# Eight of sixteen 64x64 products moved to the crosswise corners of the array, and the order of three VectorE pieces changed

## The reference

```python
qkvz = x @ W_qkvz                      # 16 key heads, each with q, k and 2 value heads, z
q, k, v = silu(causal_conv1d(...))     # 4 taps
g = cumsum(-exp(A_log) * softplus(a + dt_bias))      # within a chunk of 64 tokens
attn = -(k_beta @ k.T * decay_mask)    # strictly lower, 64x64, for each chunk and value head
for i in 1..63: attn[i] += attn[i] @ attn            # forward substitution
attn = attn + I                        # the inverse of (I - the strict lower part)
for each chunk c:                      # a recurrence over 8 chunks
    v_new = attn_c @ (v_beta - (k_beta * exp(g)) @ state)
    out_c = (q @ state) * exp(g) + tril(q @ k.T * decay) @ v_new
    state = state * exp(g_last) + (k * decay).T @ v_new
out = rmsnorm(out * silu(z)) @ W_out
```

## Time and profile before

| | |
|---|---|
| median of 3 runs | 5113.57 us (5109.58 to 5119.2) |
| the profiled execution | 5113.86 us |
| its span | 5112.0 us |
| PE busy | 4816.1 us, 94% |
| DVE busy | 3623.3 us, 71% |
| ACT busy | 3030.3 us, 59% |
| POOL busy | 1086.1 us, 21% |
| granted TensorE clock, whole span | 0.99 of full speed |

### The profile page before, as it was taken

How to read it: one execution, slowest core, us unless ns; L and a number is a source line. 1 busy time by engine, 2 the same in 40 slices (tenths; PEclk the granted TensorE clock), 3 DMA queues, 4 the chain that set the end, 5 groups by cost and what they waited for, 6 DMA issues and landing times.

```text
span 5112.0 us, 140221 instructions
## 1 busy us (share of the span) xinstructions
PE 4816.1 (94%) x52272; PEld 3343.4 (65%) x52272; DVE 3623.3 (71%) x6423; ACT 3030.3 (59%) x7915; POOL 1086.1 (21%) x1064
## 2 busy tenths in 40 slices
PE   4998999999999999999999999999999999999998
PEld 2555666666666666666666666666666666666666
DVE  7554777777777677777777777777776777777775
ACT  2333665666666566666666566666666666666665
POOL 0000222222222222222222222222222222222222
PEclk9998999999999999999999999999999999999999
DMA  2111222222222222222222222222222222222221
GB/s 59 40 43 55 65 59 55 57 61 63 59 53 74 69 59 56 56 61 63 60 53 73 70 59 54 58 61 63 59 53 71 68 62 53 58 63 57 65 52 35
DMA packets 686356, 300.71 MB, mean 59 GB/s; under 512 B 599152, under 2 KB 642288, under 8 KB 675440
## 3 DMA queue, kind: packets, MB, share of 16 engines
q1 hardware_dynamic: 546416, 283.18, 21.7%
q10 hardware_dynamic: 139264, 8.42, 1.8%
HBM read 212.76 MB, written 66.07 MB: 55 GB/s over the span
## 4 chain that ended last, share of the span: by engine, by line
issue 50%; PE 25%; POOL 12%; DVE 6%; DMA 3%; ACT 2%; ACTq 1%; SPq 1%; POOLq 0%; DVEq 0%
POOL sdec L1514 5%; PE pj L653 4%; POOL rout L1520 4%; PE dsb L790 2%; PE pot L598 2%; POOL kn L1507 2%; PE pj L648 2%; PE ms L711 2%; PE pot L748 2%; PE ms L582 1%; PE dsb L762 1%; PE pj L582 1%; PE pot L719 1%; POOL gb L1502 1%; ACTq L332 1%
## 5 line engine op out<-in xcount | busy, mean ns | idle before, releaser
L1261 DVE SCALAR_TENSOR_TENSOR cy<-xpad,cw,cy 128x1024 f32<-128x1024 f32 x768 | 1105.1, 1446 | 8.6 <-ACT cy L974 1.6
L653 PE MATMUL pj<-xnT,wt 128*128 128x512 f32 x2048 | 1021.2, 622 | 25.9 <-DMA xnT<-xnT_d 14.3
L1520 POOL TENSOR_TENSOR rout<-rin,expo 128x2 f32<-128x2 f32 x512 | 359.0, 701 | 2336.9 <-DVE rin L1402 2336.9
L1514 POOL TENSOR_TENSOR sdec<-st,gel 128x512 f32<-128x512 f32 x384 | 402.9, 1049 | 1149.5 <-DVE st L1391 970.2
L653 PEld LDWEIGHTS pj<-xnT,wt 128*128 128x128 f32 x2048 | 351.4, 191 | 355.5 <-issue 340.8
L790 PE MATMUL dsb<-wo,yT 128*128 128x256 f32 x2048 | 573.5, 402 | 8.0 <-issue 7.0
L973 ACT ACTIVATE xpad<-pj 128x512 f32<-128x512 f32 x512 | 304.1, 594 | 376.0 <-PE pj L653 376.0
L648 PE MATMUL pj<-wt,xnT 128*128 128x256 f32 x2048 | 510.2, 392 | 0.0
L1032 ACT ACTIVATE yT<-dsb 128x256 f32<-128x256 f32 x512 | 196.6, 384 | 522.3 <-PE dsb L781 522.1
L1391 DVE TENSOR_TENSOR st<-dsb,sdec 128x512 f32<-128x512 f32 x384 | 265.3, 691 | 312.9 <-PE dsb L762 312.7
L965 ACT ACTIVATE arena<-pj 128x512 f32<-128x512 f32 x256 | 152.9, 597 | 468.4 <-issue 320.3
(11 more groups left out here) (166 smaller groups left out, 8453.7 us busy)
## 6 DMA issues: line engine op xcount, KB each, us to landing
qge<-ge_rows SPq DMA_DIRECT2D x64, 1024.0 KB, 7.0
wt<-in_L_attn_W_qkvz SPq DMA_DIRECT2D x64, 768.0 KB, 4.6
gb<-g_rows SPq DMA_DIRECT2D x128, 256.0 KB, 4.1
a_d<-at SPq DMA_DIRECT2D x64, 512.0 KB, 2.6
wo<-in_L_attn_W_out SPq DMA_DIRECT2D x64, 256.0 KB, 2.7
x_d<-xpair SPq DMA_DIRECT2D x128, 128.0 KB, 1.8
ap_<-a_d SPq DMA_DIRECT2D x512, 16.0 KB, 1.8
dd<-x_d SPq DMA_DIRECT2D x512, 16.0 KB, 2.0
```

The source lines that it names most:

```text
L653: last = mm(pj[n % 2][:, :], wt[:, k, col:col + DH], batch(xnT, k, i), start=(k == 0), stop=(k == KD - 1))
L1261: stt(y, x[:, :, tap:tap + SEQ], cw[:, kind, tap:tap + 1], y, ALU.mult, ALU.add).then_inc(S["conv"], 1)
L1514: tt(sdec[:, :, :, :], st[:, c % 2, :, :, :], bc(gel[:, p, :, :].rearrange("p h (b c) -> p b h c", b=NB)[:, :, :, c], 3, DH), ALU.mult).th ...
L1520: tt(rout[:, :], rin[:, :], expo[:, 0, 0:GRP], ALU.pow).then_inc(S["routs"], 1)
```

## The change

1. Of the 16 units, the last eight go crosswise: unit 8 + v of sequence b enters the array from its own rows (b) but leaves by the columns of the other half (1 - b). So one loop step uses all four 64x64 corners: the straight product of unit v writes bank ms0, the turned product of unit 8 + v writes ms1. A turned operand lies in the other half of the partitions in the next round: odd steps turn it, even ones turn it back. That wants two more tiles: `pback`, the off x dd products of units 8 to 15 unturned, and `eturn`, their ee in the other half.
2. For `pback`, 16 more products stand in slot 19, in the two straight corners, into bank pj1 (`off_products_back`), and a third `negated` copy of 512 columns on ACT. For `eturn`, SP issues eight more DMAs of 8 KB after those of `dd`.
3. The two halves of a step are one loop now: PE waits for both additions of a round before it, and both `yp` signals come at its end.
4. On DVE the first product of the join moves from slot 14 to slot 12 (`join_first`); `join_right` and `turn_inverse` stay in slot 15 but stand right behind `residual` (`front_urgent`); `decayed_squares` of q moves from slot 15 to slot 18, also right behind `residual`; the taps of the value heads move from slots 17, 17, 18, 18, 20, 21 to 15, 15, 17, 17, 18, 20.
5. On ACT `squares` of q moves behind the ring's copies of slot 10, and `silu` of the second value head from slot 22 to 21.

```diff
-                        ("kk", 2), ("pp", 2), ("yp", 6),
+                        ("kk", 2), ("pp", 3), ("yp", 6),
...
+                loaded(sp, d_x1, g, 1)
+                apart(sp)
+                for r in range(GRP * NBLK):
+                    turned = (r + NBLK) % (GRP * NBLK)
+                    sp.dma_start(eturn[turned * BLK:(turned + 1) * BLK, :, (r % NBLK) * BLK:(r % NBLK + 1) * BLK],
+                                 x_d[r * U + U // 2:(r + 1) * U, 1].rearrange("u j i -> j u i")).then_inc(d_et, 16)
...
+            def tile_product(out, b, lhsT, rhs, a):
+                return mm(out, lhsT, rhs, start=True, stop=True, tile_position=(a * CH, b * CH))
+
-            def off_products(g, p, n):
-                if n == 0:
-                    loaded(pe, d_dd, g, GRP * NBLK)
-                    loaded(pe, d_off, g, NB * (NBLK - 1))
-                    after(pe, "atit", g, 2)
-                else:
-                    after(pe, "coef", g, 5)
+            def off_products(g, p):
+                loaded(pe, d_dd, g, GRP * NBLK)
+                loaded(pe, d_off, g, NB * (NBLK - 1))
+                after(pe, "atit", g, 2)
+                after(pe, "coef", g, 5)
                 apart(pe)
                 for v in range(8):
-                    u = 8 * n + v
+                    cut = slice(v * CH, (v + 1) * CH)
                     for b in range(NB):
-                        last = mm(ms[n][half(b), v * CH:(v + 1) * CH], off[half(b), u, :], dd[half(b), u, :],
-                                  start=True, stop=True, tile_position=(b * CH, b * CH))
-                last.then_inc(S["pp"], 1)
+                        straight = tile_product(ms[0][half(b), cut], b, off[half(b), v, :], dd[half(b), v, :], b)
+                        turned = tile_product(ms[1][half(1 - b), cut], 1 - b, off[half(b), 8 + v, :],
+                                              dd[half(b), 8 + v, :], b)
+                straight.then_inc(S["pp"], 1)
+                turned.then_inc(S["pp"], 1)
+
+            def off_products_back(g, p):
+                after(pe, "pcopy", g, RING - 4)
+                apart(pe)
+                for v in range(8):
+                    for b in range(NB):
+                        last = tile_product(pj[1][half(b), v * CH:(v + 1) * CH], b, off[half(b), 8 + v, :],
+                                            dd[half(b), 8 + v, :], b)
+                last.then_inc(S["pp"], 1)
...
+            def fixpoint(g, p, r):
                 if r == 0:
                     loaded(pe, d_ee, g, GRP * NBLK)
-                    after(pe, "pneg", g, n + 1)
+                    loaded(pe, d_et, g, GRP * NBLK)
+                    after(pe, "pneg", g, 2)
                 else:
-                    after(pe, "yadd", g, 2 * (r - 1) + n + 1)
+                    after(pe, "yadd", g, 2 * r)
+                    if r == 1:
+                        after(pe, "pneg", g, 3)
...
+                        straight = tile_product(ms[0][half(b), cut], b, pbd[half(b), v, :], src[half(b), v, :], b)
+                        if r == 1:
+                            turned = tile_product(ms[1][half(1 - b), cut], 1 - b, pback[half(b), v, :],
+                                                  yy[half(b), 8 + v, :], b)
+                        else:
+                            rhs = yy[half(1 - b), 8 + v, :] if r else eturn[half(1 - b), v, :]
+                            turned = tile_product(ms[1][half(b), cut], b, pbd[half(1 - b), 8 + v, :], rhs, 1 - b)
+                straight.then_inc(S["yp"], 1)
+                turned.then_inc(S["yp"], 1)
...
                 if s == 10:
                     silu(g, p, 1)
-                    squares(g, p, 1)
...
+                if s == 10:
+                    squares(g, p, 1)
...
-                for n, at_s in enumerate((2, 3, 3, 8, 8, 9, 17, 17, 18, 18, 20, 21)):
+                for n, at_s in enumerate((2, 3, 3, 8, 8, 9, 15, 15, 17, 17, 18, 20)):
...
+            def front_urgent(g, hk, s):
+                if s == 15:
+                    join_right(g)
+                    turn_inverse(g)
+                if s == 18:
+                    decayed_squares(g, hk % 2, 1)
...
                     if c:
                         residual(g, p, c)
+                    urgent(3 * c)
```

More of the change, by code:

```diff
@@ L108, in build @@
         pbd = sb("pbd", [P, U, CH])
+        pback = sb("pback", [P, U // 2, CH])
+        eturn = sb("eturn", [P, U // 2, CH])
         st = sb("st", [P, 2, NB, GRP, DH])
@@ L204, in build @@
         d_w, d_g, d_ge, d_wo, d_q = sem("d_w"), sem("d_g"), sem("d_ge"), sem("d_wo"), sem("d_q")
[L205 removed]
+        d_a0, d_a, d_off, d_x0, d_x1, d_dd, d_ee, d_et = (sem(n) for n in ("d_a0", "d_a", "d_off", "d_x0", "d_x1", "d_dd", "d_ee", "d_et"))
         phase = sem("phase")
@@ L708, in fixpoint @@
                 for v in range(8):
-                    u = 8 * n + v
+                    cut = slice(v * CH, (v + 1) * CH)
                     for b in range(NB):
-                        last = mm(ms[n][half(b), v * CH:(v + 1) * CH], pbd[half(b), u, :], src[half(b), u, :],
-                                  start=True, stop=True, tile_position=(b * CH, b * CH))
-                last.then_inc(S["yp"], 1)
+                        straight = tile_product(ms[0][half(b), cut], b, pbd[half(b), v, :], src[half(b), v, :], b)
[5 more added lines that the diff above has]
+                            turned = tile_product(ms[1][half(b), cut], b, pbd[half(1 - b), 8 + v, :], rhs, 1 - b)
@@ L806, in front_piece @@
                     chunk_squares(g, p, 1)
-                for n in range(2):
-                    if s == 19:
-                        off_products(g, p, n)
-                for n, at_s in enumerate((20, 20, 22, 22, 23, 23)):
+                if s == 19:
+                    off_products(g, p)
+                    off_products_back(g, p)
+                for r, at_s in enumerate((20, 22, 23)):
                     if s == at_s:
-                        fixpoint(g, p, n // 2, n % 2)
+                        fixpoint(g, p, r)
                 for n in range(RING - 2, RING):
@@ L1008, in negated @@
                     before(act, "yp", g)
-                fn(pbd[:, 8 * n:8 * n + 8, :], ms[n][:, :].rearrange("p (u c) -> p u c", u=8), ACT.Copy, scale=-1.0
+                fn(pbd[:, 8 * n:8 * n + 8, :] if n < 2 else pback[:, :, :],
+                   (ms[0], ms[1], pj[1])[n][:, :].rearrange("p (u c) -> p u c", u=8), ACT.Copy, scale=-1.0
                    ).then_inc(S["pneg"], 1)
@@ L1041, in front_piece @@
                     silu(g, p, 1)
-                    squares(g, p, 1)
                 if s == 16:
                     output_weights(g, p)
-                for n in range(2):
+                for n in range(3):
                     if s == 19:
@@ L1106, in done_then @@
                 dve.wait_ge(s, n)
-            for t in (xpad, dd, ee, off, xpair):
+            for t in (xpad, dd, ee, eturn, off, xpair):
                 dve.memset(t[:], 0.0)
@@ L1369, in add_round @@
                 src = ms[n][:, :].rearrange("p (u c) -> p u c", u=8)
+                add = eturn[:, :, :] if (r, n) == (1, 1) else ee[:, us, :]
                 if r < 2:
-                    tt(yy[:, us, :], src, ee[:, us, :], ALU.add).then_inc(S["yadd"], 1)
+                    tt(yy[:, us, :], src, add, ALU.add).then_inc(S["yadd"], 1)
                 else:
@@ L1427, in front_piece @@
                     invert_rows(g, 5, 8)
+                    join_first(g)
                 if s == 14:
                     join_left(g)
-                if s == 15:
-                    join_right(g)
-                    turn_inverse(g)
-                    decayed_squares(g, p, 1)
-                for n, at_s in enumerate((2, 3, 3, 8, 8, 9, 17, 17, 18, 18, 20, 21)):
+                for n, at_s in enumerate((2, 3, 3, 8, 8, 9, 15, 15, 17, 17, 18, 20)):
                     if s == at_s:
@@ L1439, in front_piece, with core @@
                         add_round(g, p, n // 2, n % 2)
-            def core(g, hk, fill=lambda s: None, first=False):
+            def front_urgent(g, hk, s):
[4 more added lines that the diff above has]
+                    decayed_squares(g, hk % 2, 1)
+            def core(g, hk, urgent=lambda s: None, fill=lambda s: None, first=False):
                 p = hk % 2
@@ L1468, in front @@
                 for s in range(3 * NC):
+                    front_urgent(g, hk, s)
                     front_piece(g, hk, s)
             def weave(g, hk, first=False):
-                core(g, hk, lambda s: front_piece(g + 1, (hk + 1) % HK, s), first)
+                core(g, hk, lambda s: front_urgent(g + 1, (hk + 1) % HK, s),
+                     lambda s: front_piece(g + 1, (hk + 1) % HK, s), first)
             meet(dve, 1)
```

16 lines of the change are left out of this document (8 added, 8 removed).

## The result

The changed kernel took 4975.6 us (median, 4973.1 to 4981.6); the kernel before, run beside it, 5111.6. The ratio is 0.9735, with a 95% interval of 0.9718 to 0.9752: 136 us faster, where I had forecast 170. The profiled execution took 4975.1, its span 4973.3.

A forecast was written before the change was run, and what follows sets the result against it. PE, busy 94% of the span, was taken to bound the kernel. The walked head's 2.75 us, plus 0.44 for `dd`, minus 0.5, gave 2.65 us x 64 = 170 us: 4945 us, range 4900 to 4990 (for all cases 4895 to 5085).

The forecast's parts named there:

- Packs: Four groups of 64 records a head: 1.05 us each with four corners at work, 3.75 us a head saved.
- A: Packs: four corners overlap but share a limit, 22 ns a record, 1.5 us a pack; 5035 us; chance 0.15.
- B: Packs: crosswise corners don't run beside straight ones, packs stay at 2.0 us; 5160 us, chance 0.13; extreme about 5600, chance 0.02.
- Third group: The 16 new products into pj1, in two corners: 32 records of 29 ns, 0.95 us a head of added work.
- Slot 10: ACT's ring copies go ahead of `squares`, so the second L638 doesn't wait its 0.42 us.
- chunk 5: `residual` comes 1.0 us sooner, so `solve` loses its 0.46 us wait and starts 1.0 us early.
- `dd`: `off_products` no longer waits for the DMAs of `dd`: 0.44 us a head on the mean.
- Decayed squares: Before `off_products`: new wait of 0.7 us for `decayed_squares`, the price of its move to slot 18.
- `solve` of chunks 6 and 7: PE's wait before `solve`: ready at 2170.75 but starting 2171.0 in chunk 6; new wait 0.4 us in chunk 7.
- The first round: The DMAs of `eturn` land 0.5 us before it starts, the thinnest cover; no wait counted there.
- hand-overs: Four new hand-overs between engines with nothing to spare, 0.1 to 0.2 us each: minus 0.5 us a head.
- the sum: The walked head gains 2.75 us, plus 0.44 for `dd`, minus 0.5: 2.65 us x 64 = 170 us.

The follow-up runs named there:

- the order alone: The kernel before with only VectorE's and ScalarE's new order; products, loads and copies as before: ratio 0.9802 to the kernel before.
- the early squares: The changed kernel with `decayed_squares` at the start of slot 17 and one tap a slot later: ratio 0.9650 to the kernel before.
- the corners were undone: The changed kernel with the second eight units sent straight through the same two corners as the first eight: ratio 0.9961 to the kernel before.

## Why the prediction was right, and where it was off

- **Packs.** 1.05 us forecast, 0.95 and 1.09 measured; 3.75 us a head forecast, 3.77 measured. Rivals A and B are out. A record starts every 15 ns (0.94 us from the first to the last of 64), in one corner every 58. What I called a late start of a pack is the late start of a group of another tile shape behind it. The Trainium skill's floor of about 25 ns (TensorE: Matmul & The Clock Gate, "Wait — 56ns, not 53.3ns?") doesn't hold across four corners here, nor did it across two: in the trace of before the records start in pairs 6 to 7 ns apart, and my "The 29 ns here do not contradict it" looked at the mean alone. The Trainium skill's four independent tiles (TensorEngine Tiling (Array Packing), Tiling Modes) do.
- **Third group.** 0.95 forecast, 1.07 measured, since `update` behind it has another tile shape (64*128) and starts 148 ns after its last record. Without the third group the pack before it takes 1.09 us instead of 0.95.
- **Slot 10, chunk 5, `dd`.** The waits of 0.42, 0.46 and 0.44 us went, as walked: chunk 3 lost 0.46 us and chunk 5 0.53, and the order alone brought 1.5 us a head on the mean.
- **Decayed squares.** 0.7 us of new wait forecast, 0.68 measured; the early squares showed that it was on the path in full.
- **`solve` of chunks 6 and 7.** Forecast 0.25 and 0.4 us. None in chunk 6; in chunk 7 about 0.3 us in 22 of 61 heads, 0.1 us on the mean.
- **The first round.** "Of which I count nothing": here the walk was short. Chunk 6 had 0.75 us of idle time beyond the squares on the mean. The profile partly names the turned loads; but 0.59 of the 0.75 us lie in pauses that end 1.15 to 1.55 us after an instruction piece, and leaving the loads out gained nothing. A copy of ACT cost another 0.27 us of idle time behind the second round, in 37 of 61 heads. These took the place of the 0.5 us that I had set aside for hand-overs and of the waits before `solve`.
- **A pause in the head that was walked.** "The first round ends at 2176.55, 0.8 us before it did": in the trace of before the group behind that round starts at 2177.99, 1.44 us later and not 0.8. The round had stopped in its middle:

```profile
2175.37 1.11 PE L711 MATMUL ms<-ee,pbd 64*64 64x64 f32 x30
2176.78 1.27 PE L711 MATMUL ms<-ee,pbd 64*64 64x64 f32 x34 [0.30 <-issue]
```

  It took 2.62 us, 0.6 more than the median of 2.01, and went on 1.56 us after the end of an instruction piece. The walk books these 0.6 us as gained, in each of 64 heads. But PE's idle time at the first round was 0.33 us a head on the mean before (19.9 us in 61 heads) and is no less now (19.8 us). Even with all of the 0.33 gone, the sum had 0.3 us a head too much, 18 us in all. So the pause that the change was to multiply stood in the head that I walked, as `issue` in the earlier trace rows, and I passed over it.
- **The mean.** The median head gained 2.7 us, against 2.65 in the sum. That they meet is partly luck: the 0.3 us above and the idle time of the first round were too good, the waits before `solve` of 0.65 us too bad (0.1 came). What failed besides is the step from one head to 64: "The next head's weights, issued behind them, are wanted 14 us later". At a change of pass they are not there in time, for they stand behind the store and not only behind the turned loads (without those loads the wait is still 14.8 of 20.0 us); and where the loop starts again TensorE pauses up to 6.5 us for something that the profile does not name. In chunks 7 and 0 the mean less the median, times 62, went from 28 to 59 us: that is 31 of the 34 us between forecast and result. I had read "the 64 heads look alike" off the page, and "70 to 73 us" a head; in the trace of before nine take 73.4 to 77.3, and the waits for the convolution weights and the 18.7 to 23.9 us stretches stood there too.

The split is instructive. In my sum the products gave 2.8 us a head and then lost 1.85 of it to waits (0.7, 0.25, 0.4 and 0.5); measured, at the median, 1.0 was left of 2.7. The split came out well since both parts were walked through the same head; that the total did is in part the luck told above.

## What to carry to other kernels

Products that become twice as dense also ask for instructions twice as fast: look for pauses without a releaser in the middle of a group, and at the instruction queue just before them. Multiply a walk through one head only after comparing mean and median of the heads, and look at the odd ones (a change of pass, the loop's start) by themselves. Of a change with a dense product and a new order, run each alone; here the order brought three quarters.

## What the runs showed of the hardware

- Records of 64x64 fp32 products (two records each) start every 15 ns on the mean in four 64x64 corners, every 29.5 in two, every 58 in one. A group of another tile shape started 148 to 149 ns after the last record of a pack, one of the same shape after 10 (in the kernel after) to 52 (`intra` behind the second round, before).
- TensorE's instructions come in 16 KB pieces (455 in the kernel after). 33 of its pauses of over 0.5 us, 37.0 us in all, ended 1.15 to 1.55 us after the end of such a piece; 9, with 7.1 us, where the corners were undone.
- An empty TensorE instruction took some 0.15 us in a run of 128, as long as ten records of the small products.
- A 4 KB load landed 8.2 us after its issue behind 640 KB of stores and 768 KB of weights in the same queue, and 1.8 us in the median of all heads.
- After a pause of 6.8 us TensorE's granted clock was 0.5, and the next four matmuls (128x512) took 3.8 us instead of 2.0.
